# Delta rule stage: the convolution's three older taps as fused multiply-adds on VectorE instead of scaled copies on ScalarE

## What is computed

```python
def _causal_conv_silu(x, w):
    xp = jnp.pad(x, ((0, 0), (KS - 1, 0), (0, 0)))      # KS = 4
    y = sum((xp[:, i:i + x.shape[1], :] * w[:, i] for i in range(KS)))
    return jax.nn.silu(y)
...
mixed_qkv = hidden_states @ W_qkv
mixed_qkv = _causal_conv_silu(mixed_qkv, conv_w)
q, k, v = jnp.split(mixed_qkv, [K_DIM, 2 * K_DIM], axis=-1)
...
def step(S, xs):
    q_t, k_t, v_t, g_t, b_t = xs
    S = S * jnp.exp(g_t)[..., None, None]
    kv = jnp.einsum('bhk,bhkv->bhv', k_t, S)
    S = S + jnp.einsum('bhk,bhv->bhkv', k_t, (v_t - kv) * b_t[..., None])
    o_t = jnp.einsum('bhk,bhkv->bhv', q_t, S)
```

## Time and profile before

| | |
|---|---|
| median of three runs | 2650.12 us |
| profiled execution, its own time | 2650.15 us |
| its span, first to last instruction | 2648.4 us |
| mean granted TensorE clock | 0.889 of full speed |
| TensorE matmuls busy | 2112.3 us (80%), 25432 instructions |
| VectorE busy | 1862.2 us (70%), 4409 instructions |
| ScalarE busy | 1441.6 us (54%), 2941 instructions |
| GpSimd busy | 799.0 us (30%), 852 instructions |
| the six scaled copies, L2281 | 384 instructions of 128x256, median 508 ns |

### The profile page before, as it was taken

How to read it: one execution, slowest core, us unless ns; L and a number is a source line. 1 busy time by engine, 2 the same in 40 slices (tenths; PEclk the granted TensorE clock), 3 DMA queues, 4 the chain that set the end, 5 groups by cost and what they waited for, 6 DMA issues and landing times. The chain is left out here.

```text
span 2648.4 us, 63269 instructions
## 1 busy us (share of the span) xinstructions
PE 2112.3 (80%) x25432; PEld 1309.6 (49%) x25432; DVE 1862.2 (70%) x4409; ACT 1441.6 (54%) x2941; POOL 799.0 (30%) x852
## 2 busy tenths in 40 slices
PE   2698988988888485479899888888888885677984
PEld 1244444444444264245556565555655553454652
DVE  2477777777776335688999989899998983672333
ACT  0366677677676223666666766766666543222221
POOL 1000001001001134124444444344444442104884
PEclk9599999999998797688988988998999987698997
DMA  5000000000000161100000000000000003234334
GB/s 186 37 1 1 9 5 9 5 5 9 5 5 9 33 173 47 28 10 11 13 12 12 13 12 12 13 12 12 8 8 14 5 4 97 73 109 97 44 45 88
DMA packets 109525, 85.51 MB, mean 32 GB/s; under 512 B 22366, under 2 KB 97282, under 8 KB 108976
## 3 DMA queue, kind: packets, MB, share of 16 engines
q1 hardware_dynamic: 95664, 68.31, 8.8%
q0 software_dynamic: 13568, 13.14, 3.1%
HBM read 59.22 MB, written 22.71 MB: 31 GB/s over the span
## 5 line engine op out<-in xcount | busy, mean ns | idle before, releaser
L624 ACT ACTIVATE Pr<-Pr,nmax 128x512 f32<-128x512 f32 x512 | 341.3, 714 | 173.0 <-DVE nmax L555 168.3
L729 PE MATMUL bank<-ident,Pr 128*128 128x128 f32 x2048 | 301.6, 289 | 82.5 <-DVE PT L564 64.6
L729 PEld LDWEIGHTS bank<-ident,Pr 128*128 128x128 f32 x2048 | 232.0, 147 | 254.9 <-DVE PT L564 163.4
L555 DVE CUSTOM_DVE_ANT_0 Pr<-bank,Tb 128x512 f32<-128x512 f32 x512 | 331.0, 684 | 22.9 <-PE bank L715 21.6
L564 DVE COPY PT<-bank 128x512 f32<-128x512 f32 x256 | 176.4, 689 | 176.1 <-PE bank L743 171.6
L2486 PE MATMUL bank<-Wcv,hw 128*128 128x512 f32 x512 | 261.1, 657 | 6.0 <-ACT bank L2275 5.1
L2101 DVE TENSOR_TENSOR pr<-AC,Tc 128x30 f32<-128x30 f32 (+14 forms) x480 | 212.2, 442 | 20.2 <-POOL Tc L1969 6.3
L2102 DVE TENSOR_TENSOR Tc<-Tc,pr 128x30 f32<-128x30 f32 (+14 forms) x480 | 187.6, 391 | 16.5
L631 ACT ACTIVATE PT<-bank 128x512 f32<-128x512 f32 x256 | 150.9, 590 | 71.8 <-PE bank L743 66.9
L715 PE MATMUL bank<-kp,qp 8*128 8x512 f32 x1024 | 172.5, 663 | 0.8 <-DVE nmax L555 0.8
L1918 POOL TENSOR_TENSOR Xs<-vt,Xs 128x512 f32<-128x512 f32 x64 | 80.3, 1273 | 285.4 <-DVE Xs L2011 285.3
(11 more groups left out here) (409 smaller groups left out, 4362.2 us busy)
## 6 DMA issues: line engine op xcount, KB each, us to landing
aB<-alpha SPq DMA_DIRECT2D x64, 128.0 KB, 2.8
Tb<-scores SPq DMA_DIRECT2D x1, 7168.0 KB
w<-in_L_ffn_W SPq DMA_DIRECT2D x16, 256.0 KB, 5.4
rawW<-in_L_ffn_up_w SPq DMA_DIRECT2D x16, 256.0 KB, 3.1
rawW<-in_L_ffn_gw SPq DMA_DIRECT2D x16, 256.0 KB, 3.5
rawW<-in_L_ffn_down_w SPq DMA_DIRECT2D x16, 256.0 KB, 4.3
disp<-zero SPq DMA_DIRECT2D x1, 2580.0 KB, 15.2
xin<-disp SPq DMA_DIRECT2D x8, 322.5 KB, 6.3
```

Source lines behind the costliest of these rows:

```text
L555: V.tensor_tensor_reduce(out=Pr[:, s, i, :], in0=pS[hh][:, :], in1=Tb[:, h, at:at + L], scale=-1.0, scalar=3.0e38, op0=ALU.add, op1=ALU.mi ...
L624: A_(Pr[:, s, i, :], Pr[:, s, i, :], ACT.Exp, scale=-1.0, bias=nmax[:, s, i:i + 1])\
L729: last = TR(pT[m % 2][:, t * P:(t + 1) * P], Pr[:, (G % 2) * HG + hh, t, j * P:(j + 1) * P], ident[:, :])
```

## The change

The older taps are no longer multiplied on ScalarE. VectorE takes `raw` as it is and does, for each older tap i and each column block j, one scalar_tensor_tensor: `raw` shifted by i, times the tap (a column of `cw`, one value for each partition), plus the sum so far; i = 2 and 1 write back to `BY`, i = 0 writes `yc`. The two j of a tap are issued without a wait between them; the next tap waits for both. The tile `yp` and the semaphores `a_yp` and `a_lk` are gone, `v_by` is new. The convolution waits for `BY` (semaphore `a_m`), and GpSimd's halo copy waits for the convolution, which now reads `raw`.

```diff
--- before.py
+++ after.py
@@ -1772,15 +1772,14 @@
     HF = HV // 2
     Wqk, Wcv, Wz, Wo, cw, hT, bT, gT, GC = [w[n] for n in ("Wqk", "Wcv", "Wz", "Wo", "cw", "hT", "bT", "gT", "GC")]
     with Stage(nc, ["p_ks", "p_qs", "p_w", "p_ds", "p_pu", "p_kk", "p_m",
-                    "v_ks", "v_qs", "v_s", "v_o", "v_lt", "v_at", "v_ac", "v_tt", "v_conv", "v_ss",
+                    "v_ks", "v_qs", "v_s", "v_o", "v_lt", "v_at", "v_ac", "v_tt", "v_conv", "v_by", "v_ss",
                     "v_rn", "v_rk", "p_nm", "p_nt", "a_rt", "v_sr", "v_link", "g_x", "g_s", "g_d1", "g_t", "g_t0", "g_halo", "g_on", "g_hw", "g_ac", "v_nm", "a_kq", "g_ud",
-                    "a_m", "a_w", "a_yp", "a_on", "a_sq", "a_osq", "a_or", "a_lk", "d_al0", "d_al1", "d_out",
+                    "a_m", "a_w", "a_on", "a_sq", "a_osq", "a_or", "d_al0", "d_al1", "d_out",
                     "k_y0", "k_y1", "k_y2", "k_y3", "k_m", "k_x", "k_v", "k_var", "k_rstd", "k_nm", "k_xn", "k_xT", "k_hT",
                     "k_rows", "k_be", "k_e", "k_ee", "k_al", "k_alz", "k_ad", "k_ga", "k_gb", "k_gce"]) as s:
         raw = s.sb("raw", [P, 4, 2, 4, KS - 1 + 2 * CK])
         hw = s.sb("hw", [P, 2, KS, 4, CK])
         yc = s.sb("yc", [P, 2, 2, 4, 2 * CK])
-        yp = s.sb("yp", [P, KS - 1, 2, 4, 2 * CK])
         sq = s.sb("sqc", [P, 2, 2, 2, 2, P])
         rkq = s.sb("rkq", [P, 3, 2, 2, HK])
         rq2 = s.sb("rq2", [P, 2, HK])
@@ -1950,7 +1949,7 @@
                     m, tp = t // 4 + 1, t % 4
                     if m == NP:
                         return
-                    pool.wait_ge(s["a_yp"], t + 1)
+                    pool.wait_ge(s["v_conv"], t + 1)
                     if m % (NP // 2) == 0:
                         G.memset(raw[:, tp, :, :, 0:KS - 1], 0.0).then_inc(s["g_halo"], 1)
                     else:
@@ -2060,14 +2059,21 @@
                     V.transpose(rkT[:, :], rkd[:, :, :].rearrange("p e h -> p (e h)"))
 
                 def conv(t):
-                    dve.wait_ge(s["a_yp"], t + 1)
-                    flat = lambda x: x.rearrange("p j x t -> p (j x t)")
-                    link(V.tensor_tensor(BY[:, :], BY[:, :], flat(yp[:, 2, :, :, :]), ALU.add))
-                    link(V.tensor_tensor(BY[:, :], BY[:, :], flat(yp[:, 1, :, :, :]), ALU.add))
-                    if t >= 2:
-                        dve.wait_ge(s["a_kq"], t - 1)
-                    V.tensor_tensor(flat(yc[:, t % 2, :, :, :]), BY[:, :], flat(yp[:, 0, :, :, :]), ALU.add)\
-                        .then_inc(s["v_conv"], 1)
+                    tp = t % 4
+                    dve.wait_ge(s["a_m"], done("pj", t))
+                    for i in (2, 1, 0):
+                        if i == 0 and t >= 2:
+                            dve.wait_ge(s["a_kq"], t - 1)
+                        for j in range(2):
+                            acc = BY[:, 256 * j:256 * j + 256].rearrange("p (x t) -> p x t", x=4)
+                            last = V.scalar_tensor_tensor(acc if i else yc[:, t % 2, j, :, :],
+                                                          raw[:, tp, j, :, i:i + 2 * CK],
+                                                          cw[:, TILE[2 * tp + j], i:i + 1], acc, ALU.mult, ALU.add)
+                            if i:
+                                last.then_inc(s["v_by"], 1)
+                        if i:
+                            dve.wait_ge(s["v_by"], 4 * t + 2 * (3 - i))
+                    last.then_inc(s["v_conv"], 1)
 
                 def attend(c):
                     m, e = c // 2, c % 2
@@ -2267,19 +2273,14 @@
                     act.wait_ge(s["p_m"], done("pj", t))
                     act.wait_ge(s["g_halo"], t + 1)
                     bank = M[USE[("pj", t)] % 2][:, :].rearrange("p (j x t) -> p j x t", j=2, x=4)
-                    A_(raw[:, tp, :, :, KS - 1:KS - 1 + 2 * CK], bank, ACT.Copy).then_inc(s["a_lk"], 1)
+                    A_(raw[:, tp, :, :, KS - 1:KS - 1 + 2 * CK], bank, ACT.Copy)
                     if t:
                         act.wait_ge(s["v_conv"], t)
-                    tap = lambda j, i: cw[:, TILE[2 * tp + j], i:i + 1]
+                    tap = lambda j: cw[:, TILE[2 * tp + j], KS - 1:KS]
                     for j in range(2):
                         last = A_(BY[:, 256 * j:256 * j + 256].rearrange("p (x t) -> p x t", x=4), bank[:, j, :, :],
-                                  ACT.Copy, scale=tap(j, KS - 1))
+                                  ACT.Copy, scale=tap(j))
                     last.then_inc(s["a_m"], 1)
-                    act.wait_ge(s["a_lk"], t + 1)
-                    for i in (2, 1, 0):
-                        for j in range(2):
-                            last = A_(yp[:, i, j, :, :], raw[:, tp, j, :, i:i + 2 * CK], ACT.Copy, scale=tap(j, i))
-                    last.then_inc(s["a_yp"], 1)
 
                 def squash(t):
                     act.wait_ge(s["v_conv"], t + 1)
```

## The result

The changed kernel takes 2691.6 us, the median of four runs (2689.3 to 2704.3), against 2650.2 before: 41 us or 1.6% slower by the medians. The ratio over all runs is 1.0178 with a 95% interval of 1.015 to 1.0205. The profiled execution took 2689.26 us, with a span of 2687.5 against 2648.4, so 39.1 us are to be found in the traces. (One of the four runs of before took 3965 us; it is left out of the ratio.)

The account below looks back on a forecast made before the run. The prediction took VectorE to bound the kernel and summed 2650.2 + 37.1 (convolution) + 28.2 (GpSimd holds) - 17.5 (recovered waits) = 2698 us, +1.8%. Its range was 2645 to 2730 us.

Parts of the forecast that it names:

- the steps' sum: Whole kernel: +37.1 us for VectorE's convolution, +28.2 for GpSimd holds, -17.5 for recovered waits.
- the likeliest case: Whole kernel: dearer convolution and new GpSimd holds outweigh recovered waits, 2698 us, +1.8%; chance 0.54.
- The bound, and a wait that is worth nothing: Delta rule stage: VectorE is the bound; removing its commonest wait for TensorE gives nothing, 18.35 against 18.40 us.
- The price: VectorE's convolution: six instructions of 486 ns, a tile 2.63 us instead of 2.06, +37.1 us over 64 tiles.
- rival C: VectorE's convolution: GpSimd holds the new instructions too, through the pointer in SBUF; 60 us on top, 2758 us; chance 0.10.
- rival D: VectorE's convolution: the new instructions run at half throughput, +102 us, 2800 us; chance 0.03.
- The lead-in and the first steps: Ahead of the steps and in the first two: VectorE's waits behind ScalarE's copies shrink, -4.4 and -6.7 us.
- The moved holds: Odd steps: earlier Ud and S multiplication on GpSimd hold VectorE's substitution, net 2.35 us in each of 12, +28.2.
- the term I had priced at 28.2: Odd steps: net cost of GpSimd's earlier Ud and S multiplication holding VectorE's substitution, 2.35 us in each of 12.
- -6.4: Later steps: VectorE's waits that go, 4.4 us in odd steps, about 1 in even steps, about 1 at step 16.

Follow-up runs that it names:

- e5: The changed kernel with a constant 0.25 in place of the tap's column as scalar of VectorE's six instructions; 2665.3 us.
- e1: The changed kernel with ScalarE's six scaled copies put back into a tile that nobody reads; 2667.3 us.
- e3: The changed kernel with GpSimd's second Ud in odd steps waiting for the first instruction of VectorE's second convolution; 2652.3 us.
- e8: The changed kernel with only GpSimd's second S multiplication in odd steps waiting for the second convolution's first instruction, Ud staying early; 2671.2 us.
- e2: The kernel before with ScalarE's six copies made for tile 0 alone, VectorE's work unchanged; 2637.6 us.
- e6: The kernel before, in even steps with norms behind the convolution on VectorE and GpSimd's second S multiplication ahead of Tc's preparation; 2607.7 us.

## Why the prediction was right

Forecast were 2698 us with the steps' sum of +47.8; it became 2691.6, +41.4, and the likeliest case came. Step by step:

*The bound, and a wait that is worth nothing.* Right, by a balance that is taken apart below. The 30.7 us of waits in the earlier trace rows are gone, and the way from the AC transpose to the read-out is as long as in the earlier trace rows.

*The price.* 486 ns and 2.63 us a tile were said, 483 ns and 2.61 us are measured; 64 x 0.55 = 35 us instead of 37.1. e5 shows that 60 ns of each instruction are the column. The new instructions are not held (446 to 502 ns, all 384), so rival C is out; rival D too, with no instruction near 750 ns. The rule cited for D speaks of two SBUF sources; the new instruction reads one tensor from SBUF, so it concerns this change only if the column counts as a source. ScalarE's busy time fell by 148 us, not 160.

*The lead-in and the first steps.* Right in kind, too small. Both waits of 3.3 us became 0.88 (0.9 said), here at tile 3:

```profile
1089.02 1.41 DVE L2069 SCALAR_TENSOR_TENSOR bank<-raw,cwq,bank 128x256 f32<-128x256 f32 x3 [0.88 <-ACT bank L2281]
```

From the first mark to step 2 there are 14 tiles, +7.7 us by the measured price, and the stretch shortened by 7.1. So 14.8 us came back where I had 11.1. With the six copies kept (e1) the same stretch takes 182.3.

*The moved holds.* The chain came in the order written, with one link wrong. Ws is 1.5 us earlier relative to the read-out of the step shown (2.15 said). The prediction had TensorE not keep it back, by the earlier trace rows; but TensorE's solve starts 3.5 us behind the read-out instead of 2.6, ScalarE's first Ws follows it at 4.74 instead of 3.81, and that 0.9 us is carried down the chain. (Over the 12 steps Ud is 2.2 us earlier on average, 12.8 to 10.6, since the kernel before had later ones.) The rest: the two holds are 0.72 and 1.58 = 2.30 us (2.75 said), 0.23 less at the first Ud (0.4 said), so 2.07 net instead of 2.35, the second convolution at 14.19 (14 to 14.5 said). e1, e3 and e8 show that these holds are a cause beside the price; e2 shows that the relief alone doesn't bring them in this size.

*What the sum didn't have.* The 13 pairs came out at +52.1, and I had 50 x 0.58 + 28.2 - 6.4 = +50.8 for them. That agreement is luck; two errors nearly cancel: a term that is 16 us too large and one of 19 us that is missing. Groups of VectorE in these 13 pairs (busy, mean ns, idle), before and then after:

```profile
L2101 DVE TENSOR_TENSOR pr<-AC,Tc 128x228 f32<-128x228 f32 x26 | 16.2, 625 | 0.4
L2038 DVE TENSOR_TENSOR nrm<-nrm,rkq 128x16 f32<-128x16 f32 x26 | 14.6, 562 | 0.9
L2102 DVE TENSOR_TENSOR Tc<-Tc,pr 128x238 f32<-128x238 f32 x26 | 10.6, 407 | 0.9
```

```profile
L2108 DVE TENSOR_TENSOR Tc<-Tc,pr 128x238 f32<-128x238 f32 x26 | 29.6, 1138 | 0.9
L2107 DVE TENSOR_TENSOR pr<-AC,Tc 128x228 f32<-128x228 f32 x26 | 10.2, 393 | 0.4
L2037 DVE TENSOR_TENSOR nrm<-nrm,rkq 128x16 f32<-128x16 f32 x26 | 5.3, 204 | 0.9
```

By such groups the account is this. The new instructions: 50 tiles x 0.55 = +27.5. The two 238-column instructions are held for 27.6 us more, 19.0 of them in the second, which is the term I had priced at 28.2 with the relief. But holds also went: -9.3 at the nrm multiplication, which the late S multiplication had hit before, and -11.2 at the 228- and 234-column instructions; 5.3 came at others (210, 220 and 198 columns +8.0, gate and norms part -2.7). So the net of the moved holds is 12.4, not 28.2: I followed one kind of step and one place, and didn't ask what the same instructions were holding where they stood. The waits for TensorE ahead of S took 30.7 us away, and 26.2 of it were given back, 18.3 as waits for Tc and 7.9 as longer holds on the 30- to 84-column instructions behind, with 4.0 us less in small waits elsewhere: -8.5, where I had -6.4. Last, the new wait for the read-out, which I didn't have: +18.8. The sum, 27.5 + 12.4 - 8.5 + 18.8, is 50.2 of 52.1; the rest is spread. Of the 8.7 us between 47.8 and the traces' 39.1, 6.2 are the earlier start of the stage, which is chance, and 4.1 the lead, less 1.6 in the pairs and behind.

## What to carry over

When one engine is the bound, relieving another isn't always free: ask what its earlier results set off, and whether that runs into the bound engine's work; here 148 us less on ScalarE, together with the longer convolutions, moved two GpSimd instructions from under the convolution onto the substitution. By itself the same relief cost nothing in total (e2). Where an instruction that reads two SBUF tensors stands beside GpSimd work, place it, or the GpSimd work, by order or by one added wait; that was worth more (39 us in e3, 41 in e6) than the arithmetic that was moved. Ask too what the moved work held where it stood before. And check a forecast that sums up well term by term, since errors cancel.

## What the runs showed of the hardware

- A multiply-add on VectorE with a column as its scalar takes 483 ns for 128x256, with a constant 423; it isn't held by GpSimd although the column and one tensor lie in SBUF (446 to 502 ns over 384 instructions).
- With two fp32 tensors in SBUF the same kind of instruction isn't slower than an add (0.69 us for 512 columns). The Trainium skill (Vector Engine (DVE) Microarchitecture Reference, "Points that are easy to get wrong") has half throughput for it; the measurement decides.
- GpSimd's multiplications of SBUF tensors hold VectorE's instructions with two SBUF tensors for up to their whole duration: 1.99 us for one of 0.41 beside an S multiplication of 2.06. Two SBUF inputs aren't the only case. The copy rkd<-rkq, which reads one SBUF tensor and writes another, takes 0.17 us alone; in the changed kernel it was issued at 1505.29 beside an S multiplication of 1.95 us from 1505.18, and lasted 1.88 us.
- Behind 4 us in which TensorE did nothing its granted clock was 0.50 for 7 us, and 16 products took 4.96 us; with the gap filled by eight useless products it was 1.00, the same products took 3.63 us, and the kernel was 12 to 14 us faster.
